# Table lookups by one-hot matmul: two float32r parts of three tables in place of three bfloat16 parts of four

## The chip, the cores and the metric

One core of a Trainium2 chip runs the whole kernel. The metric is device microseconds of one execution, outside the profiler; the engines are called TensorE (PE, with PEld for its weight loads), VectorE (DVE), ScalarE (ACT), GpSimd (POOL) and SyncE (SP), as the profile's abbreviations have them.

## What is computed

A recommender's pairwise attention over 26 embedded fields, for a batch of 2048:

```python
emb = jax.vmap(lambda tbl, idx: tbl[idx], in_axes=(0, 1), out_axes=1)(embed_tables, sparse)   # 2048 x 26 x 32
bi = emb[:, FIRST, :] * emb[:, SECOND, :]                     # 325 pairs of fields
a = jax.nn.relu(jnp.einsum('bpd,dh->bph', bi, att_w_w) + att_w_b)
scores = jnp.einsum('bph,ho->bpo', a, att_d_w) + att_d_b
att_weight = jax.nn.softmax(scores, axis=1)
att_out = jnp.sum(att_weight * bi, axis=1)
x = jnp.concatenate([att_out, dense], axis=-1)
out = jax.nn.sigmoid(x @ fin_w + fin_b)
```

Each of the 26 tables has 12,500 rows of 32 float32 values (128 bytes a row). All is float32.

## The kernel before

The batch is 16 tiles of 128 rows, worked in four *quads* of four tiles (`g` is the tile in the quad). A quad runs over the fields f = 0 to 25. Field f's rows for the four tiles stand side by side in `emb[:, f, :]`, are transposed by VectorE (L829 into PSUM as `turned`, L831 into SBUF as `emb_t`), and multiplied with all fields before f (L855); the products go into a ring of six groups of 16 pairs. TensorE multiplies each full group twice, by the attention weights (L491) and by the final weights (L501), both in float32 on four column tiles of 32; ScalarE applies the relu (L614) and TensorE reduces it to scores (L515). At a quad's end stand the softmax's maximum, exponentials and weighted sums (L891 to L946).

The rows of `emb` come in by three ways, and the change shifts work between them:

- **Gathers.** GpSimd issues one indirect DMA of 128 rows for each tile and field (L441), in the order of the fields. `gathers_of(f)` (L125) says how many of a quad's four tiles are gathered: 4 as a rule, fewer where another way serves a field. From the second quad on, GpSimd waits before field f until VectorE has transposed field f of the quad before (L435); so it can be up to one quad ahead. That makes 352 gathers, and L430 issues one more for field 24: 353.
- **Row copies.** For two tiles of field 24, SyncE copies single rows by their register addresses (L411): 128 DMAs a tile, 7 tiles (`TILES_SP`), 896 DMAs. The addresses are loaded 32 at a time (L407, 28 loads). ScalarE sets the rows into `emb` before field 24 (L656, `place_rows`).
- **Lookups.** Four fields (`LOOK = (3, 9, 15, 19)`) are looked up by TensorE: all four tiles of fields 3, 9 and 15, two tiles of field 19 (`LOOK_TILES`), 14 tiles a quad. The table lies in SBUF as 128 x 7 chunks of 14 rows; a one-hot matrix of the chunk numbers (L750, VectorE) times the table picks for each batch row its chunk of 14 x 32 = 448 values in PSUM (L476); `take_looked` masks the row wanted (L840) and sums over the 14 (L843). To be exact, the float32 table is split into three bfloat16 parts: `make_high` (L587, ScalarE rounds), `make_rest` (L757, VectorE subtracts), `make_middle` (L592, ScalarE rounds the rest), `make_low` (L762, VectorE subtracts). A tile takes 7 chunks x 3 parts = 21 matmuls, in two steps (chunks 0 to 3, chunks 4 to 6).

The order on TensorE is written out by hand: `STEP_FIELDS` lists beside which field each of a quad's lookup steps stands, and the first table of the next quad is looked up beside the end of this one. Before the first field, field 3 of quad 0 is looked up. SyncE loads the tables (L377 to L380): the first two at the start, the other two between its row copies, each after a wait that the ring's space, in which the raw table lies, has become free.

Of the kernel before, what the change touches and what calls it, by code (L numbers as in the profile page):

```python
# [5 lines left out]
P = 128  # L6
G = 4
# [16 lines left out]
LOOK = (3, 9, 15, 19)  # L24
LOOK_TILES = (4, 4, 4, 2)
CHUNKS = 7
CHUNK_ROWS = 14
PART_ROWS = CHUNKS * CHUNK_ROWS
CHUNK_DT = mybir.dt.float16
PARTS = 3  # L30
STEPS = (slice(0, 4), slice(4, 7))
STEP_FIELDS = (1, 2, 2, 3, 4, 4, 5, 6, 6, 7, 8, *range(8, 21), 22, 24)
SPLIT_FIELD = {2: 4, 3: 8}
# [14 lines left out]
def attention_fm(nc, dense, sparse, tables, params, look_index, sp_index, chunk_numbers, out):  # L48
    f32, i32, bf16 = mybir.dt.float32, mybir.dt.int32, mybir.dt.bfloat16
# [132 lines left out]
    with ctx:  # L182
# [19 lines left out]

        look_parts = sb("look_parts", [P, LOOKS, CHUNKS, PARTS, CHUNK_ROWS * D], bf16)

# [9 lines left out]
        onehot = sb("onehot", [P, CHUNKS, G * P], bf16)  # L214
# [75 lines left out]
        look_rest_made = [sem(f"look_rest_made{n}") for n in range(len(LOOK))]  # L290
        look_middle_made = [sem(f"look_middle_made{n}") for n in range(len(LOOK))]
# [73 lines left out]
        def _(sp):  # L365
# [27 lines left out]
            for q in range(QUADS):  # L393
                for i in range(PLACED - TILES_SP[q], PLACED):
# [3 lines left out]
                    for p in range(0, P, ROWS_SP):  # L398
# [5 lines left out]
                        if tiles == 0 and p == P // 2:  # L404
                            sp.wait_ge(look_low_made[1], len(STEPS))
                            load_table(3)
# [40 lines left out]
        def _(pe):  # L447
# [12 lines left out]
            for q in range(QUADS):  # L460

                def look_up(i):
                    of, n, g, part = steps[i]
                    made = (look_high_made[n], look_middle_made[n], look_low_made[n])
# [110 lines left out]
        def _(act):  # L575
# [14 lines left out]
            def make_middle(n, part):  # L590
                act.wait_ge(look_rest_made[n], part + 1)
                nc.scalar.activation(look_parts[:, n, STEPS[part], 1, :], raw[n][:, STEPS[part]], ACT.Copy  # L592
                                     ).then_inc(look_middle_made[n], 1)

# [6 lines left out]
            make_middle(0, 0)  # L601
            make_middle(0, 1)
            make_high(1, 0)
            make_high(1, 1)
            make_middle(1, 0)
            make_middle(1, 1)
            for q in range(QUADS):
# [51 lines left out]
                for f in range(1, F):  # L659
                    if f == SP_PLACE:  # L660
                        place_rows()
                    if q == 0:
                        for n in range(2, LOOKS):
                            for part in range(len(STEPS)):
                                if f == SPLIT_FIELD[n] - 1:
                                    make_high(n, part)
                                if f == SPLIT_FIELD[n] + 1:
                                    make_middle(n, part)
# [26 lines left out]
        def _(dve):  # L695
# [323 lines left out]
```

## Time and profile before

| | |
|---|---|
| runs, median | 479.75 us (478.36 to 480.0, 3 runs) |
| profiled execution, its span | 755.4 us; the page has no other time for it |
| TensorE busy | 489.4 us, 2788 instructions, mean granted clock 0.837 |
| VectorE busy | 419.0 us, 692 instructions |
| GpSimd busy | 343.8 us, 357 instructions |
| ScalarE busy | 118.3 us, 218 instructions |
| DMA moved | 15.60 MB in 15495 packets |

The profiled execution is one execution with the hardware profiler on; here it is over half as long again as the runs without it. A group's busy time is the sum of its instructions' durations; the number after the comma is the mean of one. TensorE's instructions overlap, so that its pace is read from the distance of starts, not from the duration of one. In the chain that ended last each row is a start, a length and what ran; "issue" is time in which nothing was waited for. In a timeline row the brackets hold the engine's idle time before and what ended it.

### The profile page before, as it was taken

The numbers are of one execution on the slowest core, as the hardware profiler recorded it, in microseconds if no ns is written. First come the engines' busy times: TensorE is split into PE (matmuls) and PEld (weight loads), VectorE is DVE, ScalarE is ACT, GpSimd is POOL, SyncE is SP. The second block draws the span as 40 slices with busy tenths as digits, with TensorE's granted clock in tenths as the row PEclk, the third lists the DMA queues.
The fourth block names the chain that finished last, engine by engine and source line by source line (L and its number), as shares of the span: only waits on it lengthen the run. The fifth ranks groups of instructions, "written<-read, shape, count | busy, mean of one in ns | idle before, by whom it ended". The sixth has DMA issues, their size and how long they took to land.

```text
span 755.4 us, 9968 instructions
## 1 busy us (share of the span) xinstructions
PE 489.4 (65%) x2788; PEld 175.7 (23%) x2788; DVE 419.0 (55%) x692; ACT 118.3 (16%) x218; POOL 343.8 (46%) x357
## 2 busy tenths in 40 slices
PE   2853102136686888737696898647687989999516
PEld 0321000012222233312232233212222224433102
DVE  6943003047475656444485666254476666899616
ACT  4211000003011123000011132000012132013114
POOL 6777777624745441744564541744564640000000
PEclk9985555559888899958898999868898999999958
DMA  7532521201211111111221110121221210000000
GB/s 234 120 18 13 99 13 12 13 3 9 13 8 12 8 10 33 12 8 10 11 11 10 10 10 4 13 37 9 11 12 9 12 10 2 2 2 2 0 1 1
DMA packets 15495, 15.60 MB, mean 21 GB/s; under 512 B 8177, under 2 KB 14161, under 8 KB 15057
## 3 DMA queue, kind: packets, MB, share of 16 engines
q0 software_dynamic: 11296, 5.81, 14.3%
q1 hardware_dynamic: 3488, 8.38, 3.1%
q10 hardware_dynamic: 656, 0.79, 0.4%
q8 instruction: 22, 0.36, 0.2%
q14 instruction: 33, 0.26, 0.1%
HBM read 14.93 MB, written 0.02 MB: 20 GB/s over the span
## 4 chain that ended last, share of the span: by engine, by line
SPq 59%; issue 38%; DVE 1%; PE 1%; DMA 1%; ACT 1%; ACTq 0%
SPq L411 51%; SPq L407 7%; DMA index<-look_index 0%; PE sums_s L515 0%; DVE ring L855 0%; PE sums_f L501 0%; PE first L491 0%; ACT score L685 0%; SPq L380 0%; DVE neg_max_early L891 0%; DMA emb_placed<-tables 0%; SPq L385 0%; ACT second_s L627 0%; ACT hidden L614 0%; PE back_s L538 0%
## 5 line engine op out<-in xcount | busy, mean ns | idle before, releaser
L441 POOL DMA_INDIRECT emb<-tables,rows x308 | 294.0, 955 | 261.0 <-DVE emb_t L831 164.6
L476 PE MATMUL looked_own<-look_parts,onehot 128*128 128x448 bf16 x735 | 178.8, 388 | 119.3 <-issue 75.3
L855 DVE TENSOR_TENSOR ring<-emb_t,turned 128x512 f32<-128x512 f32 (+9 forms) x180 | 193.9, 1114 | 3.4
L476 PE MATMUL back_s<-look_parts,onehot 128*128 128x448 bf16 x441 | 100.5, 380 | 73.2 <-issue 49.7
L614 ACT ACTIVATE hidden<-first,par 128x512 f32<-128x512 f32 (+1 forms) x84 | 56.4, 677 | 507.8 <-PE first L491 304.6
L476 PEld LDWEIGHTS looked_own<-look_parts,onehot 128*128 128x128 bf16 x735 | 72.7, 104 | 229.4 <-issue 158.9
L491 PE MATMUL first<-ring,par 128*32 128x512 f32 (+1 forms) x672 | 105.7, 616 | 22.6 <-DVE ring L855 8.2
L501 PE MATMUL sums_f<-ring,par 128*32 128x512 f32 (+1 forms) x672 | 105.7, 605 | 5.1 <-issue 4.2
L840 DVE TENSOR_TENSOR look_masked<-back_s,look_mask 128x448 f32<-128x448 f32 x21 | 13.0, 621 | 125.0 <-remote 70.8
L750 DVE TENSOR_TENSOR onehot<-chunk_of,turned 128x2048 bf16<-128x2048 f16 (+3 forms) x30 | 53.0, 1767 | 43.0 <-PE looked_own L476 26.4
L476 PEld LDWEIGHTS back_s<-look_parts,onehot 128*128 128x128 bf16 x441 | 43.6, 103 | 137.6 <-issue 79.8
L840 DVE TENSOR_TENSOR look_masked<-looked_own,look_mask 128x448 f32<-128x448 f32 x35 | 21.7, 621 | 96.2 <-remote 62.0
L441 POOL DMA_INDIRECT emb<-tables,rows_first x44 | 47.9, 1089 | 16.4 <-issue 13.1
L829 DVE STREAM_TRANSPOSE turned<-emb 128x128 f32<-128x128 f32 x100 | 31.9, 319 | 41.1 <-ACT emb L656 41.0
L515 PE MATMUL sums_s<-hidden,par 128*32 128x512 f32 (+1 forms) x168 | 29.0, 651 | 25.4 <-ACT hidden L614 25.4
L501 PEld LDWEIGHTS sums_f<-ring,par 128*32 128x32 f32 x672 | 26.4, 114 | 63.9 <-issue 61.8
L491 PEld LDWEIGHTS first<-ring,par 128*32 128x32 f32 x672 | 18.5, 109 | 74.9 <-issue 55.8
L843 DVE TENSOR_REDUCE emb<-look_masked 128x32 f32<-128x448 f32 x56 | 34.7, 620 | 1.9
L831 DVE STREAM_TRANSPOSE emb_t<-emb 128x128 f32<-128x128 f32 x100 | 27.1, 271 | 0.0
L592 ACT ACTIVATE look_parts<-ring 128x1792 bf16<-128x1792 f32 (+1 forms) x8 | 11.6, 1501 | 38.8 <-issue 26.2
L757 DVE TENSOR_TENSOR ring<-ring,look_parts 128x1792 f32<-128x1792 f32 (+1 forms) x8 | 14.1, 1790 | 3.5 <-issue 2.9
L515 PEld LDWEIGHTS sums_s<-hidden,par 128*32 128x32 f32 x168 | 5.6, 116 | 42.5 <-ACT hidden L614 34.2
(71 smaller groups left out, 145.0 us busy)
## 6 DMA issues: line engine op xcount, KB each, us to landing
emb_placed<-tables SPq DMA_DIRECT2D x896, 0.1 KB
emb<-tables,rows POOLq DMA_INDIRECT x308
ring<-tables SPq DMA_DIRECT2D x3, 1568.0 KB
chunk_of<-chunk_numbers SPq DMA_DIRECT2D x3, 512.0 KB, 3.6
ring<-tables SPq DMA_DIRECT2D x1, 896.0 KB
emb<-tables,rows_first POOLq DMA_INDIRECT x44
ring<-tables SPq DMA_DIRECT2D x1, 672.0 KB
chunk_of<-chunk_numbers ACTq DMA_DIRECT2D x1, 384.0 KB, 3.9
```

The costliest lines, as they stand in the source:

```text
L407: _, at = nc.values_load_multi_w_load_instructions(sp_rows[t:t + 1, p:p + ROWS_SP], engines=(mybir.EngineType.SP,), min_val=0, max_val=F * ...
L411: sp.dma_start(emb_placed[p + k:p + k + 1, q, i * D:(i + 1) * D], stacked[bass.ds(at[k], 1), :]).then_inc(sp_gathered[tiles], 16)
L441: pool.indirect_dma_start(emb[:, f, g * D:(g + 1) * D], None, stacked, bass.IndirectOffsetOnAxis(ap=row, axis=0), element_offset=at,).then ...
L476: mm = nc.tensor.matmul(looked_rows[look_bank[tile]], onehot[:, c, g * P:(g + 1) * P], look_parts[:, n, c, k, :], start=c == 0 and k == 0, ...
L491: mm = nc.tensor.matmul(first[gr % 2][j * TILE:(j + 1) * TILE, 0:n * P], w, ring[:, gr % RING, 0:n, j, :], start=True, stop=True)
L501: mm = nc.tensor.matmul(sums_f[j * TILE:(j + 1) * TILE, 0:pairs_c(gr) * P], row, ring[:, gr % RING, 0:pairs_c(gr), j, :], start=e == 0, st ...
L515: mm = nc.tensor.matmul(sums_s[tile * TILE:(tile + 1) * TILE, cut], d_sel[:, half, :], hidden[:, gr % HIDDEN, cut], start=half == 0, stop= ...
L614: nc.scalar.activation(hidden[:, gr % HIDDEN, cut], first[gr % 2][:, cut], ACT.Relu, bias=par[:, cols["bias_a"]]).then_inc(relu_done, 1)
L750: nc.vector.tensor_tensor(onehot[:, chunks, tiles], numbers.unsqueeze(1).broadcast_to(shape), here[:, chunks].unsqueeze(2).broadcast_to(sh ...
L840: nc.vector.tensor_tensor(look_masked[:], looked_rows[look_bank[tile]].rearrange("p (i d) -> p d i", d=D), mask, ALU.mult).then_inc(look_m ...
L843: nc.vector.tensor_reduce(emb[:, LOOK[n], g * D:(g + 1) * D], look_masked[:], AX.X, ALU.add).then_inc(look_summed, 1)
L855: nc.vector.tensor_tensor(slot[:, at:at + n, :], emb_t[:, i:i + n, :], turned[:, f % 2, :].unsqueeze(1).broadcast_to((P, n, P)), ALU.mult) ...
```

## The change

The tables are split into two parts of type float32r in place of three of bfloat16, and the one-hot matrix is float32r too. `make_rest` and `make_middle` go; `make_low` subtracts the high part from the raw table and writes the low part. A part has twice the bytes of before, so that two parts of three tables take the memory of three parts of four: field 19 is no longer looked up, and all four of its tiles are gathered. A quad has 12 looked-up tiles of 14 matmuls. `STEP_FIELDS` is drawn up anew for 22 + 2 steps. The descriptor memory for DMAs issued by GpSimd is set to 8192 bytes, where it had the default.

```diff
-LOOK = (3, 9, 15, 19)
-LOOK_TILES = (4, 4, 4, 2)
+LOOK = (3, 9, 15)
+LOOK_TILES = (4, 4, 4)
...
-PARTS = 3
+PARTS = 2
 STEPS = (slice(0, 4), slice(4, 7))
-STEP_FIELDS = (1, 2, 2, 3, 4, 4, 5, 6, 6, 7, 8, *range(8, 21), 22, 24)
-SPLIT_FIELD = {2: 4, 3: 8}
+STEP_FIELDS = (1, 2, 2, 3, 4, 4, 5, 6, 7, 8, 9, 10, 11, 12, 13, 13, 15, 17, 18, 20, 21, 23)
+SPLIT_FIELD = {2: 4}
+DMA_SCRATCH = 8192
...
-        look_parts = sb("look_parts", [P, LOOKS, CHUNKS, PARTS, CHUNK_ROWS * D], bf16)
+        look_parts = sb("look_parts", [P, LOOKS, CHUNKS, PARTS, CHUNK_ROWS * D], f32r)
...
-        onehot = sb("onehot", [P, CHUNKS, G * P], bf16)
+        onehot = sb("onehot", [P, CHUNKS, G * P], f32r)
...
-                        if tiles == 0 and p == P // 2:
-                            sp.wait_ge(look_low_made[1], len(STEPS))
-                            load_table(3)
...
-                    made = (look_high_made[n], look_middle_made[n], look_low_made[n])
+                    made = (look_high_made[n], look_low_made[n])
...
-            def make_middle(n, part):
-                act.wait_ge(look_rest_made[n], part + 1)
-                nc.scalar.activation(look_parts[:, n, STEPS[part], 1, :], raw[n][:, STEPS[part]], ACT.Copy
-                                     ).then_inc(look_middle_made[n], 1)
...
-            def make_rest(n, part):
+            def make_low(n, part):
                 dve.wait_ge(look_high_made[n], part + 1)
-                nc.vector.tensor_tensor(raw[n][:, STEPS[part]], raw[n][:, STEPS[part]], look_parts[:, n, STEPS[part], 0, :],
-                                        ALU.subtract).then_inc(look_rest_made[n], 1)
-
-            def make_low(n, part):
-                dve.wait_ge(look_middle_made[n], part + 1)
-                nc.vector.tensor_tensor(look_parts[:, n, STEPS[part], 2, :], raw[n][:, STEPS[part]],
-                                        look_parts[:, n, STEPS[part], 1, :], ALU.subtract).then_inc(look_low_made[n], 1)
+                nc.vector.tensor_tensor(look_parts[:, n, STEPS[part], 1, :], raw[n][:, STEPS[part]],
+                                        look_parts[:, n, STEPS[part], 0, :], ALU.subtract).then_inc(look_low_made[n], 1)
...
-    nc = bacc.Bacc("TRN2", target_bir_lowering=False, num_devices=1)
+    nc = bacc.Bacc("TRN2", target_bir_lowering=False, num_devices=1, dynamic_dma_scratch_size=DMA_SCRATCH)
```

## Rows read from the trace of the kernel before

**Rows 1.** The page: span, busy time, TensorE's clock, the chain's shares.

```profile
span 755.4 us, 9968 instructions
...
PE 489.4 (65%) x2788; PEld 175.7 (23%) x2788; DVE 419.0 (55%) x692; ACT 118.3 (16%) x218; POOL 343.8 (46%) x357
...
PEclk9985555559888899958898999868898999999958
...
SPq L411 51%; SPq L407 7%; DMA index<-look_index 0%; PE sums_s L515 0%; DVE ring L855 0%; PE sums_f L501 0%; PE first L491 0%; ACT score L685 0%; SPq L380 0%; DVE neg_max_early L891 0%; DMA emb_placed<-tables 0%; SPq L385 0%; ACT second_s L627 0%; ACT hidden L614 0%; PE back_s L538 0%
```

**Rows 2.** The chain that ended last: start, length; SyncE's register loads.

```profile
639.59 2.17 SPq L407
...
732.36 1.16 DMA emb_placed<-tables
```

**Rows 3.** The starts of GpSimd, SyncE and VectorE's fields (timeline, chain).

```profile
3.76 1.08 POOL L441 DMA_INDIRECT emb<-tables,rows_first  x1 [3.29 <-DVE rows_first L704]
...
8.04 2.07 SPq L407
...
37.59 0.30 DVE L831 STREAM_TRANSPOSE emb_t<-emb 128x128 f32<-128x128 f32 x1
```

**Rows 4.** Timeline of the end: field 24 placed, field 25 transposed.

```profile
733.63 0.26 ACT L656 ACTIVATE emb<-emb_placed 128x64 f32<-128x64 f32 x1 [26.44 <-DMA emb_placed<-tables]
...
740.98 0.32 DVE L829 STREAM_TRANSPOSE turned<-emb 128x128 f32<-128x128 f32 x1
```

**Rows 5.** Timeline of GpSimd where it waits for nothing.

```profile
79.75 0.94 POOL L441 DMA_INDIRECT emb<-tables,rows  x1 [0.30 <-issue]
81.00 0.94 POOL L441 DMA_INDIRECT emb<-tables,rows  x1 [0.30 <-issue]
```

**Rows 6.** Waits of GpSimd: us in total, times, longest.

```profile
POOL emb L441 <- DVE emb_t L831: 164.6, 27, 16.2
```

**Rows 7.** Groups by form, GpSimd's gathers: busy us, mean ns.

```profile
L441 POOL DMA_INDIRECT emb<-tables,rows x308 | 294.0, 955 | 261.0 <-DVE emb_t L831 164.6 <-issue 84.8 <-DVE turned L829 11.6
L441 POOL DMA_INDIRECT emb<-tables,rows_first x44 | 47.9, 1089 | 16.4 <-issue 13.1 <-DVE rows_first L704 3.3
L430 POOL DMA_INDIRECT emb_placed<-tables,rows x1 | 1.6, 1628 | 0.3 <-issue 0.3
```

**Rows 8.** Stretch of quad 3: PE, PEld, DVE, ACT, POOL busy, clock, DMA.

```profile
640.00:707.00 67.00, 65.36 (x450) 24.68 (x448) 62.51 (x97) 12.51 (x19) 0.00 (x0) 1.00 0.01 1
```

**Rows 9.** Timeline of TensorE's weight loads, two looked-up tiles.

```profile
473.95 3.88 PEld L476 LDWEIGHTS back_s<-look_parts,onehot 128*128 128x128 bf16 x21
...
477.92 2.56 PEld L476 LDWEIGHTS looked_own<-look_parts,onehot 128*128 128x128 bf16 x14
```

**Rows 10.** The same, two float32 groups.

```profile
690.30 0.13 PEld L491 LDWEIGHTS first<-ring,par 128*32 128x32 f32 x4 [0.30 <-issue]
...
691.16 0.13 PEld L515 LDWEIGHTS sums_s<-hidden,par 128*32 128x32 f32 x4 [0.30 <-ACT hidden L614]
```

**Rows 11.** Groups by form, VectorE; and one row of its timeline.

```profile
L843 DVE TENSOR_REDUCE emb<-look_masked 128x32 f32<-128x448 f32 x56 | 34.7, 620 | 1.9
...
L855 DVE TENSOR_TENSOR ring<-emb_t,turned 128x2048 f32<-128x2048 f32 x12 | 27.4, 2280 | 0.0
...
L750 DVE TENSOR_TENSOR onehot<-chunk_of,turned 128x2048 bf16<-128x2048 f16 x11 | 25.1, 2283 | 15.3 <-PE looked_own L476 15.2
L840 DVE TENSOR_TENSOR look_masked<-looked_own,look_mask 128x448 f32<-128x448 f32 x35 | 21.7, 621 | 96.2 <-remote 62.0 <-issue 17.0 <-PE looked_own L476 13.2
...
L750 DVE TENSOR_TENSOR onehot<-chunk_of,turned 128x1024 bf16<-128x1024 f16 x4 | 4.9, 1221 | 27.7 <-remote 16.5 <-PE looked_own L476 11.2
...
L750 DVE TENSOR_TENSOR onehot<-chunk_of,turned 128x768 bf16<-128x768 f16 x4 | 3.8, 944 | 0.0
...
L757 DVE TENSOR_TENSOR ring<-ring,look_parts 128x1792 f32<-128x1792 f32 (+1 forms) x8 | 14.1, 1790 | 3.5 <-issue 2.9 <-ACT look_parts L587 0.5
...
32.94 3.54 DVE L762 TENSOR_TENSOR look_parts<-ring,look_parts 128x1792 bf16<-128x1792 f32 x2
```

More of the change, by code:

```diff
@@ L48, in attention_fm @@
 def attention_fm(nc, dense, sparse, tables, params, look_index, sp_index, chunk_numbers, out):
-    f32, i32, bf16 = mybir.dt.float32, mybir.dt.int32, mybir.dt.bfloat16
+    f32, i32, f32r = mybir.dt.float32, mybir.dt.int32, mybir.dt.float32r
     ALU, ACT, AX = mybir.AluOpType, mybir.ActivationFunctionType, mybir.AxisListType
@@ L289, in attention_fm @@
         look_high_made = [sem(f"look_high_made{n}") for n in range(len(LOOK))]
-        look_rest_made = [sem(f"look_rest_made{n}") for n in range(len(LOOK))]
-        look_middle_made = [sem(f"look_middle_made{n}") for n in range(len(LOOK))]
         look_low_made = [sem(f"look_low_made{n}") for n in range(len(LOOK))]
@@ L600, in _ @@
             act.wait_ge(par_in, 16)
-            make_middle(0, 0)
-            make_middle(0, 1)
             make_high(1, 0)
             make_high(1, 1)
-            make_middle(1, 0)
-            make_middle(1, 1)
             for q in range(QUADS):
@@ L666, in _ @@
                                     make_high(n, part)
-                                if f == SPLIT_FIELD[n] + 1:
-                                    make_middle(n, part)
                     done = groups_of(f)
@@ L752, in make_onehots @@
                                         ).then_inc(onehot_made, 1)
-            def make_rest(n, part):
+            def make_low(n, part):
                 dve.wait_ge(look_high_made[n], part + 1)
-                nc.vector.tensor_tensor(raw[n][:, STEPS[part]], raw[n][:, STEPS[part]], look_parts[:, n, STEPS[part], 0, :],
-                                        ALU.subtract).then_inc(look_rest_made[n], 1)
-            def make_low(n, part):
-                dve.wait_ge(look_middle_made[n], part + 1)
-                nc.vector.tensor_tensor(look_parts[:, n, STEPS[part], 2, :], raw[n][:, STEPS[part]],
-                                        look_parts[:, n, STEPS[part], 1, :], ALU.subtract).then_inc(look_low_made[n], 1)
+                nc.vector.tensor_tensor(look_parts[:, n, STEPS[part], 1, :], raw[n][:, STEPS[part]],
+                                        look_parts[:, n, STEPS[part], 0, :], ALU.subtract).then_inc(look_low_made[n], 1)
             make_onehots(0, 0, 0)
-            make_rest(0, 0)
             make_onehots(0, 0, 1)
-            make_rest(0, 1)
             make_low(0, 0)
@@ L867, in _ @@
                                 if tile == 0:
-                                    make_rest(1, part)
-                                if tile == 1:
                                     make_low(1, part)
@@ L875, in _ @@
                                 if f == SPLIT_FIELD[n]:
-                                    make_rest(n, part)
-                                if f == SPLIT_FIELD[n] + 1:
                                     make_low(n, part)
```

## The prediction, written before the changed kernel was run

> **What bounds the kernel now.** The page's head comes first, because the time cannot be read from it directly: the profiled execution spans 755.4 us [rows 1] and the page gives it no other time, while the median of the runs is 479.75 us. So 276 us exist only under the profiler, and the first task is to find which rows still hold without it. The chain that ended last is SyncE's queue almost throughout: its two lines, 896 row copies of L411 and 28 register loads of L407, hold 58% of it, and nearly all the rest is the gaps between them [rows 1]. Late in the span, when GpSimd has nothing left to do, its steps become regular: six batches of 32 rows pass in (732.36 - 639.59) / 6 = 15.46 us each [rows 2], a register load of 2.17 us and so (15.46 - 2.17) / 32 = 0.415 us a row. I take 15.46 us as the pace without disturbance. SyncE starts at 8.04 [rows 3], so it needs 8.0 + 28 x 15.46 + some 2.5 us (an estimate, half a microsecond each) for the five table and chunk loads between = 443.4, 1.2 for the last row to land [rows 2], and 21.9 from field 24 in place (733.6) to the end (755.4) [rows 4]: 466.5 us.
>
> GpSimd next. Where it is not held it starts a gather every 1.25 us (79.75, 81.00), 0.945 busy and 0.30 before the next [rows 5]; in the profile it also waits 164.6 us in 27 places for VectorE to free a field's slot [rows 6], which is there because SyncE holds up the whole rest. Without those waits: 3.8 to its start [rows 3], busy 294.0 + 47.9 + 1.6 = 343.5 for 353 gathers [rows 7], 352 x 0.305 = 107.4 between; it ends at 454.7. About 1.2 to land (a row's landing) and 14.4 from field 25's transpose (740.98) to the end [rows 4]: 470 us.
>
> TensorE and VectorE last. From 640 to 707 quad 3 runs fields 0 to 23 with all data there: TensorE is busy 65.36 of 67.00 at a granted clock of 1.00 (2.4 GHz), VectorE 62.51 [rows 8]. That stretch has 10 looked-up tiles; quads 0 to 2 have 14, as they also make field 3 of the next quad. A tile of 21 matmuls takes 3.97 us (473.95 to 477.92) [rows 9], so four tiles are 16. Quad 3: 67.0 and 21.9 for the end = 89; quads 1 and 2: 105; quad 0, from VectorE's first field at 37.6 [rows 3], 105 + 14 of table splitting: it ends at 157. Sum 157 + 105 + 105 + 89 = 456 us.
>
> So three chains lie within 14 us of each other, GpSimd's longest: 470, 466.5, 456. All are short of 479.75. I put the 9.8 us left to what lies around the span, which no row here shows; the three are compared with each other, and the difference is laid on the median.
>
> **The change part by part.**
>
> *GpSimd.* Field 19 loses its table, so `gathers_of(19)` goes from 2 to 4: 2 more gathers in each of 4 quads, 353 to 361. At 1.25 us they are +10.0 us on a queue that in my reading never waits. What they free: nothing on this engine. Field 19 comes late by 2.5 us more per quad, and everything behind it on that queue too.
>
> *Descriptor memory.* It is set to 8192 bytes. Whether GpSimd ever waits for room there is not visible. Below: nothing, most gathers take 0.945. Above: a first-fields gather has a mean of 1089 ns against 955 for the others [rows 7]; if all 361 paid that 0.14, +50 us. I take nothing, as the undisturbed row is the one that repeats; a gain has no source, as the gathers already go back to back.
>
> *TensorE.* 14 tiles x 21 matmuls become 12 x 14 a quad: 1176 to 672. The price of one float32r matmul is on no row. From below: the bfloat16 matmul of the same shape and line, 3.97 / 21 = 0.189 us [rows 9]. From above: a float32 product of 512 columns comes as two instructions; a group of eight on four column tiles takes 0.86 us (690.30 to 691.16) [rows 10], so 448 columns would be 0.75, and half of it, one instruction, 0.376. I take 0.189, the row with the same tile and shape: a tile costs 2.65 us. A quad falls from 55.6 to 31.8 us of lookups. The new `STEP_FIELDS` lays 22 half tiles over fields 1 to 23, where 26 lay over 1 to 24. All of it lies beside GpSimd's 112 us a quad, so it is worth nothing while GpSimd is last. At 0.376 a tile costs 5.26 and a quad's lookups 63 us, 7.6 more than now; 4 quads put the TensorE chain at 456 + 30 = 486 before the splitting saved below, 468 after it, still under GpSimd's 480.
>
> The row of float32 shows 512 columns in 0.43 us per instruction, twice the time per column of bfloat16. The Trainium skill (SBUF — State Buffer, section "A bandwidth-pool intuition that's wrong (but worth ruling out)") puts TensorE's moving read at about 614 GB/s, stated for 2-byte data; 448 x 128 elements of 4 bytes would by it take an estimated 374 ns. It agrees with that row and speaks against this change: by it the lookups would cost more than before, and the sum would still be GpSimd's.
>
> *VectorE.* Gone: 8 `make_rest` (14.1 us), 2 of 8 `make_low` of the same size (3.5), the one-hots of the fourth table (4.9 + 3.8), and 8 of 56 `take_looked` at 0.62 + 0.62 (9.9) [rows 11]: 36.2 us of 419.0. The one-hots that stay write 4-byte elements; from below the row of today, 2.28 us for 2048, from above twice that, 24 x 2.0 = 48 us more. I take today's, because the float32 product of 2048 also takes 2.28 [rows 11]. `make_low` now waits for `make_high` itself; behind it stand the masks of the first tiles, and it comes earlier than today by the two steps that are gone.
>
> *ScalarE.* 8 `make_middle` and 2 `make_high` go, some 15 us on an engine busy 118.3 of 755.4 [rows 1]. It is never last; nothing.
>
> *SyncE.* One table load with its wait for `look_low_made[1]` goes, and the chunk loads shrink: under 1 us. Behind that wait stand 26 x 32 row copies, but the low part of table 1 is ready at 32.94 + 3.54 = 36.5 us [rows 11], before SyncE comes to it at 8 + 2 x 15.5 = 39; so it costs nothing today. SyncE's chain: 466.
>
> Sum: GpSimd 470 + 10 = 480, SyncE 466, TensorE and VectorE 456 - 18 of splitting - 3 quads x some 11 = 405. A quad's 105 would lose 24 of lookups, but VectorE's busy time, 419.0 - 36.2 with some 30 before the first field, leaves 88 a quad, and with its waits at a quad's end I keep 94. The longest grows by 10.0 us: 479.75 + 10 = 489.75, I say 489.5.
>
> **The rivals.** (1) *SyncE is last, GpSimd has slack.* For: its chain is only 3.5 us shorter, and an error of 1% in GpSimd's pitch turns the order. Against: SyncE's steady pace was itself taken under the profiler. It decides at a pitch of 1.22: 361 x 1.22 in place of 361 x 1.25 brings GpSimd's 480 to 469, within 2.5 of SyncE. Below that the ten microseconds vanish in the slack: 479 us, no change.
>
> (2) *TensorE and VectorE are last today.* It needs both queues to be faster than their rows: the 0.30 between gathers to shrink to 0.20 (1.15 a gather) and a copied row from 0.415 to 0.385. Then GpSimd after the change needs 480 - 361 x 0.10 = 444 and SyncE 466.5 - 896 x 0.03 = 440, and the TensorE chain, 456 plus stalls of some 8 for one-hots and masks, would have set today's time with 16 around it. After the change it no longer does: 444 + 16 = 460 us, faster. The point from which it decides is a pitch of 1.22 with SyncE as quick. For: TensorE is busy 489 us in the profile, more than the whole unprofiled time, part of it at the low clock [rows 1]. Against: in the dense stretch that clock is 1.00 [rows 8], and SyncE's copies, in regular steps there, show little added by tracing.
>
> (3) *float32r costs as float32*, 0.75 us a matmul: 10.5 us a tile, 48 x 10.5 = 504 us of lookups against 222; TensorE's chain 456 + 282 - 18 = 720, with the 9.8 around it 730 us. For: the elements have four bytes. Against: float32 comes as two instructions, and float32's is already the price of two passes over the same columns.
>
> **How the numbers follow.** Forecast 0.61, rival 1 0.16, rival 2 0.19, rival 3 0.04. A measurement of this kernel can tell about 0.5% (2.4 us) from no change. Faster 0.19, same 0.16, slower 0.65. The forecast's own range is 484 to 498: +4 where SyncE's chain takes most of it up, +18 if the 4-byte matmul and the descriptor memory add some microseconds. With rival 1 and the near side of rival 2 the range is 473 to 498.
>
> **What would show it.** The page after: 361 gathers at an unchanged pitch of 1.25, 672 lookup matmuls at 0.19 (0.38 or 0.75 by the others), `make_rest` gone, SyncE's steps of 15.46 unchanged. The profiled span should stay near 755, as SyncE's disturbed queue sets it; only the runs' time tells the chains apart. A time under 477 means that GpSimd's queue was not last; one over 500 that the float32r matmuls or the descriptor memory were priced too low.

## The result, and the profile after

| | runs, median | ratio to the kernel before | span of the profiled execution |
|---|---|---|---|
| before | 478.64 us (477.63 to 480.86, 12 runs) | | 476.3 us (a second profile) |
| after | 481.17 us (480.13 to 482.19, 12 runs) | 1.0050 (1.0036 to 1.0064) | 480.3 us |

The change makes the kernel slower by 0.5%, 2.5 us. The forecast was 489.5: the sign came true, and the size was a quarter of the one forecast (+2.5 where +10 was). 481.17 lies below the forecast's own range, 484 to 498; only the wider range, made for the rivals, holds it.

The execution profiled of the kernel before was stretched to 755.4 us [rows 1]. Profiled a second time it spans 476.3 us, in a run of 478.1; all comparisons below are with this second profile. The head of its page and its chain:

```profile
span 476.3 us, 9968 instructions
...
PE 424.1 (89%) x2788; PEld 166.1 (35%) x2788; DVE 418.2 (88%) x692; ACT 119.4 (25%) x218; POOL 346.4 (73%) x357
...
PE 50%; DVE 26%; issue 8%; POOL 7%; ACT 2%; DMA 2%; POOLq 0%; DVEq 0%
```

The same three parts of the page after:

```profile
span 480.3 us, 8890 instructions
...
PE 370.7 (77%) x2284; PEld 182.2 (38%) x2284; DVE 384.4 (80%) x654; ACT 105.5 (22%) x208; POOL 346.6 (72%) x365
...
POOL 69%; issue 22%; DMA 3%; DVE 3%; PE 2%; ACT 1%; POOLq 0%
```

TensorE is busy 53 us less, VectorE 34 us less, and GpSimd, with eight gathers more, 0.2 us more. The chain was one of TensorE and VectorE; now it is GpSimd's gathers from end to end. The waits say the same. VectorE's waits for gathers, before (second profile):

```profile
DVE turned L829 <- DMA emb<-tables,rows: 7.1, 5, 1.9
```

and after, with GpSimd's own waits:

```profile
DVE turned L807 <- DMA emb<-tables,rows: 65.8, 42, 3.5
...
POOL emb L437 <- issue: 108.5, 356, 0.3
...
POOL emb L437 <- DVE emb_t L809: 0.9, 3, 0.3
```

VectorE waits 65.8 us in 42 places where it waited 7.1 in 5: all that the lookups gave back has become waiting for gathers. GpSimd, once it has started, waits for VectorE 0.9 us in all; it issues from its first gather to its last, as the forecast had it. So the start of the last gather should tell the time. Timeline of GpSimd, the last one before (second profile) and after:

```profile
456.42 0.94 POOL L441 DMA_INDIRECT emb<-tables,rows  x1 [0.30 <-issue]
```

```profile
459.02 0.94 POOL L437 DMA_INDIRECT emb<-tables,rows  x1 [0.31 <-issue]
```

It starts 2.60 us later, and the medians of the times are 2.53 us apart. The two executions that were profiled lie further apart, 478.1 and 482.13, because 18.9 us stand behind the last gather's end before, and 20.3 after. TensorE in that stretch, before (second profile), then TensorE and VectorE after:

```profile
456.20 1.07 PE L491 MATMUL first<-ring,par 128*32 128x512 f32 x8 [0.28 <-DVE ring L855]
```

```profile
456.90 1.93 PE L487 MATMUL first<-ring,par 128*32 128x512 f32 x8 [1.67 <-DVE ring L833]
458.61 1.83 PE L497 MATMUL sums_f<-ring,par 128*32 128x512 f32 x8
...
464.75 1.22 DVE L865 TENSOR_REDUCE neg_max_early<-score 128x4 f32<-128x1024 f32 x1 [1.24 <-ACT score L629]
```

After the change the granted clock is 0.50 (1.2 GHz) from 453.4 to 460.2, behind a stretch in which TensorE had been idle for 2.46 us; the groups of eight matmuls take nearly twice as long, and VectorE waits 1.24 us for the scores that come of them. All twelve runs of the changed kernel have a lower mean clock (0.92 to 0.96) than the kernel before has in its runs (0.97 to 0.99). How much of the 2.53 us this makes is not shown; what follows is about the queue of gathers. Eight gathers at 1.25 us make 10.0, so 7.4 us must have gone from GpSimd's queue elsewhere. The groups by form show where from: gathers before (second profile), then after.

```profile
L441 POOL DMA_INDIRECT emb<-tables,rows x308 | 294.6, 956 | 93.9 <-issue 93.0 <-DVE emb_t L831 0.9
L441 POOL DMA_INDIRECT emb<-tables,rows_first x44 | 50.7, 1152 | 16.4 <-issue 13.1 <-DVE rows_first L704 3.3
```

```profile
L437 POOL DMA_INDIRECT emb<-tables,rows x316 | 298.4, 944 | 96.3 <-issue 95.4 <-DVE emb_t L809 0.9
L437 POOL DMA_INDIRECT emb<-tables,rows_first x44 | 47.0, 1069 | 16.5 <-issue 13.1 <-DVE rows_first L689 3.4
```

308 gathers fall from 956 to 944 ns in the mean (3.7 us), the 44 of the first fields from 1152 to 1069 (3.7 us): together the 7.4 that was missing. No gather became faster; a few slow ones went. GpSimd's timeline after, and VectorE's in the same microseconds:

```profile
10.23 0.94 POOL L437 DMA_INDIRECT emb<-tables,rows_first  x1 [0.31 <-issue]
11.48 2.47 POOL L437 DMA_INDIRECT emb<-tables,rows_first  x1 [0.30 <-issue]
14.25 1.16 POOL L437 DMA_INDIRECT emb<-tables,rows_first  x1 [0.30 <-issue]
15.71 0.94 POOL L437 DMA_INDIRECT emb<-tables,rows_first  x1 [0.30 <-issue]
```

```profile
9.45 1.75 DVE L735 TENSOR_TENSOR onehot<-first,par 128x1536 fp32r<-128x1536 f32 x1
11.11 3.48 DVE L742 TENSOR_TENSOR look_parts<-ring,look_parts 128x1792 fp32r<-128x1792 f32 x2
14.51 0.37 DVE L753 TENSOR_SCALAR clamped<-ids 128x416 f32<-128x416 int32 x1
```

The gathers at 11.48 and 14.25 take 2.47 and 1.16 us where their neighbours take 0.94, and both meet `make_low`, whose two operands (`ring` and `look_parts`) lie in SBUF. The one-hot of 1.75 us just before has one operand in PSUM (`first`), and the gather at 10.23 runs through it undelayed. Nearly all the time over 0.945 us stands at such places: at the sixteen `make_rest` and `make_low` before (12.7 us), at the six `make_low` after (5.2). I call what a gather takes above 0.945 us *held*, and sum it over all gathers, by the timeline's rows with their 0.01 us: 13.4 us before, 6.0 after, again 7.4 between them.

The float32r matmul is in TensorE's timeline (weight loads, two tiles of 14):

```profile
261.07 2.76 PEld L472 LDWEIGHTS back_s<-look_parts,onehot 128*128 128x128 f32 x14 [0.71 <-issue]
263.84 2.86 PEld L472 LDWEIGHTS looked_own<-look_parts,onehot 128*128 128x128 f32 x14
```

A tile takes 263.84 - 261.07 = 2.77 us, 0.198 a matmul, and the next one 2.86, 0.204, against 0.189 of bfloat16 [rows 9].

### The profile page after: what moved, and what is told of

Its sections match the earlier page's. It is cut to its first block, busy times and chain, and to the rows that moved or that the text cites. A ratio compares the mean times of both kernels' runs of the same rounds, so it can differ in the third digit from the quotient of the medians.

```text
span 480.3 us, 8890 instructions
## 1 busy us (share of the span) xinstructions
PE 370.7 (77%) x2284; PEld 182.2 (38%) x2284; DVE 384.4 (80%) x654; ACT 105.5 (22%) x208; POOL 346.6 (72%) x365
## 4 chain that ended last, share of the span: by engine, by line
POOL 69%; issue 22%; DMA 3%; DVE 3%; PE 2%; ACT 1%; POOLq 0%
POOL emb L437 68%; DMA emb<-tables,rows 2%; DVE ring L833 1%; PE first L487 1%; PE sums_f L497 1%; DMA ids<-sparse 0%; PE sums_s L511 0%; DVE turned L807 0%; ACT score L670 0%; POOLq L183 0%; DVE neg_max_early L865 0%; DVE emb_t L809 0%; POOL emb_placed L426 0%; ACT second_s L614 0%; PE back_s L534 0%
## 5 line engine op out<-in xcount | busy, mean ns | idle before, releaser
L487 PE MATMUL first<-ring,par 128*32 128x512 f32 (+1 forms) x672 | 97.0, 657 | 45.9 <-DVE ring L833 45.6
L472 PE MATMUL looked_own<-look_parts,onehot 128*128 128x448 f32 x420 | 104.8, 398 | 32.2 <-DVE onehot L735 14.7
L472 PEld LDWEIGHTS looked_own<-look_parts,onehot 128*128 128x128 f32 x420 | 81.6, 201 | 67.4 <-issue 37.0
L497 PE MATMUL sums_f<-ring,par 128*32 128x512 f32 (+1 forms) x672 | 95.8, 640 | 0.0
L807 DVE STREAM_TRANSPOSE turned<-emb 128x128 f32<-128x128 f32 x100 | 32.3, 323 | 70.1 <-DMA emb<-tables,rows 65.8
L472 PE MATMUL back_s<-look_parts,onehot 128*128 128x448 f32 x252 | 58.6, 378 | 17.8 <-DVE onehot L735 11.1
L472 PEld LDWEIGHTS back_s<-look_parts,onehot 128*128 128x128 f32 x252 | 45.7, 189 | 36.7 <-DVE onehot L735 18.3
L437 POOL DMA_INDIRECT emb<-tables,rows_first x44 | 47.0, 1069 | 16.5 <-issue 13.1
L735 DVE TENSOR_TENSOR onehot<-chunk_of,turned 128x2048 fp32r<-128x2048 f16 (+1 forms) x22 | 44.3, 2014 | 6.7 <-PE looked_own L472 6.7
L821 DVE TENSOR_REDUCE emb<-look_masked 128x32 f32<-128x448 f32 x48 | 29.8, 620 | 1.6
L583 ACT ACTIVATE look_parts<-ring 128x1792 fp32r<-128x1792 f32 (+1 forms) x6 | 8.8, 1507 | 16.1 <-DMA ring<-tables 16.0
L818 DVE TENSOR_TENSOR look_masked<-back_s,look_mask 128x448 f32<-128x448 f32 x18 | 11.1, 617 | 0.0
L614 ACT ACTIVATE second_s<-sums_s,par 128x512 f32<-128x512 f32 x12 | 8.3, 689 | 11.7 <-PE sums_s L511 11.7
```

The costliest lines, as they stand in the source:

```text
L437: pool.indirect_dma_start(emb[:, f, g * D:(g + 1) * D], None, stacked, bass.IndirectOffsetOnAxis(ap=row, axis=0), element_offset=at,).then ...
L472: mm = nc.tensor.matmul(looked_rows[look_bank[tile]], onehot[:, c, g * P:(g + 1) * P], look_parts[:, n, c, k, :], start=c == 0 and k == 0, ...
L487: mm = nc.tensor.matmul(first[gr % 2][j * TILE:(j + 1) * TILE, 0:n * P], w, ring[:, gr % RING, 0:n, j, :], start=True, stop=True)
L497: mm = nc.tensor.matmul(sums_f[j * TILE:(j + 1) * TILE, 0:pairs_c(gr) * P], row, ring[:, gr % RING, 0:pairs_c(gr), j, :], start=e == 0, st ...
L735: nc.vector.tensor_tensor(onehot[:, chunks, tiles], numbers.unsqueeze(1).broadcast_to(shape), here[:, chunks].unsqueeze(2).broadcast_to(sh ...
L807: tr = nc.vector.transpose(turned[:, f % 2, :], emb[:, f, :])
```

## The experiments

In one table what all runs gave. "Held" is the sum defined above, "waits" VectorE's for gathers of `rows`, as in the lines above. These and the last gather are of the one execution profiled, whose time lies up to 1.6 us from the median. The ratio is to the kernel before, run on the same chip in turn.

| kernel | gathers | last gather starts | held | waits | time | ratio (95%) |
|---|---|---|---|---|---|---|
| before, profiled again | 353 | 456.4 | 13.4 | 7.1 | 478.1 | |
| after | 361 | 459.0 | 6.0 | 65.8 | 481.17 | 1.0050 (1.0036 to 1.0064) |
| e1 three tables, bf16 | 361 | 463.1 | 10.1 | 53.9 | 486.37 | 1.0141 (1.0119 to 1.0164) |
| e2 two parts of three | 353 | 455.8 | 12.7 | 27.8 | 479.75 | 0.9997 (0.9979 to 1.0015) |
| e3 descriptor memory | 353 | 457.6 | 14.5 | 7.0 | 479.61 | 1.0005 (0.9988 to 1.0022) |
| e4 subtraction twice, SBUF | 361 | 460.7 | 7.6 | 59.8 | 483.65 | 1.0078 (1.0059 to 1.0098) |
| e5 the second from PSUM | 361 | 458.4 | 5.4 | 57.7 | 480.08 | 1.0019 (1.0002 to 1.0037) |
| e6 subtraction from PSUM | 361 | 454.7 | 1.7 | 61.2 | 476.5 | 0.9926 (0.9906 to 0.9945) |
| e7 before, no subtractions | 353 | 445.3 | 2.3 | 13.5 | 468.45 | 0.9762 (0.9744 to 0.9779) |
| e8 before, splits in PSUM | 353 | 449.1 | 6.1 | none | 477.85 | 0.9956 (0.9938 to 0.9973) |
| e9 after, in pieces | 361 | 456.9 | 3.9 | 66.4 | 479.02 | 0.9988 (0.9976 to 0.9999) |
| e10 before, in pieces | 353 | 450.8 | 7.7 | none | 473.93 | 0.9877 (0.9860 to 0.9894) |

**The kernel before, profiled again.** No edit.

> The kernel before, unchanged, for a second profile. The first one spans 755 us, and if the profiler happens to leave this one alone its span should be within 2 us of 478.6, as the changed kernel's is (480.3 beside 481.2). Theory A, TensorE and VectorE set the time of before: GpSimd ends its 353 gathers near 450 us, VectorE reaches the last fields later than their gathers land and waits for lookups, not for gathers; TensorE is busy over 95% in most of the span. Theory B, SyncE sets it: VectorE waits for field 24's copied rows at the quads' ends. Theory C, GpSimd sets it and its gathers were slower with the larger descriptor memory: gathers stand about 1.27 us apart and the last one lands near 462.

The span is 476.3 us and the time 478.1; the rows stand above. Only 1.8 us lie around the span. The chain of the page is that of theory A, while the gathers, 1.29 us apart in the mean, are rather those of theory C; its cause, the descriptor memory, is tried below.

**Three tables without float32r.** The gathers of the change alone: its table list, its steps and its loads, with three bfloat16 parts.

```diff
-LOOK = (3, 9, 15, 19)
-LOOK_TILES = (4, 4, 4, 2)
+LOOK = (3, 9, 15)
+LOOK_TILES = (4, 4, 4)
...
-                        if tiles == 0 and p == P // 2:
-                            sp.wait_ge(look_low_made[1], len(STEPS))
-                            load_table(3)
```

> Before with the three tables, 12 tiles and 361 gathers of the change, but still three bfloat16 parts. Theory A: TensorE loses 8 of 56 tiles (32 us of lookups), so GpSimd becomes last as in the changed kernel: 480.5 to 482, the float32r parts are then worth nothing. Theory B: the same, 481. Theory C: 478.6 + 10 = 488.6.

None of the three theories had it: the time grows by 6.8 us (486.37 against 479.59). On GpSimd's queue: +10.0 for eight gathers, -3.3 held, as the fourth table's four subtractions are gone; the last gather starts 6.6 us later. So the gathers cost what the forecast said, and the two float32r parts, which take six more subtractions away, give the rest back.

**Two parts of three.** A third of the lookup matmuls left out of the kernel before; all splitting stays.

```diff
-                    for k in range(PARTS):
+                    for k in range(PARTS - 1):
...
-                                                  stop=c == CHUNKS - 1 and k == PARTS - 1)
+                                                  stop=c == CHUNKS - 1 and k == PARTS - 2)
```

> Before with the third part's matmuls left out (14 instead of 21 a tile; the tables are still split in three, so the lowest part is missing from the looked-up rows); 353 gathers. Theory A: TensorE loses 392 matmuls, 74 us, and GpSimd's 353 gathers set the time: 481.2 - 8 x 1.25 = 471, 1.6% faster. Theory B and theory C: 478.6, no change.

Theory A's 471 is missed: 392 matmuls fewer change nothing (0.9997). GpSimd's last gather starts at 455.8, and VectorE's waits for gathers grow from 7.1 to 27.8 us. TensorE's chain is not the one that limits alone, for all that the page names it in the chain.

**Descriptor memory.** The kernel before with the change's setting.

```diff
-    nc = bacc.Bacc("TRN2", target_bir_lowering=False, num_devices=1)
+    nc = bacc.Bacc("TRN2", target_bir_lowering=False, num_devices=1, dynamic_dma_scratch_size=8192)
```

> Before with the descriptor memory of 8192 bytes alone. Theory A and theory B: 478.6, no change. Theory C: about 471, as the gathers get their 1.25 us.

1.0005, with the long gathers still where the subtractions are. The setting is not their cause, and theory C is out.

**The subtraction once more, with both operands in SBUF.** The changed kernel, with each `make_low` preceded by one of the same size into a spare tensor.

```diff
             def make_low(n, part):
                 dve.wait_ge(look_high_made[n], part + 1)
+                dve.wait_ge(spare_made, n * len(STEPS) + part)
...
+                nc.vector.tensor_tensor(spare, raw[n][:, STEPS[part]], look_parts[:, n, STEPS[part], 0, :], ALU.subtract
+                                        ).then_inc(spare_made, 1)
```

> The changed kernel with each of the six subtractions of make_low done once more into unused memory: both operands in SBUF, 10.7 us of VectorE in all. Theory L (GpSimd's gather is held up while VectorE subtracts two SBUF tensors): the gathers' time over 0.945 us each, 6.0 us in all in the changed kernel, about doubles to 11 to 12, the last gather starts 5 us later (464) and the time is 486. Theory M (the table loads' DMA traffic slows the early gathers): the excess stays at 6, the time 481.2. Theory N (VectorE's own time matters at the start): later first field by some 7 us, but the time stays within 1 us, as GpSimd is last.

**The same, with one operand in PSUM.** The edit is shown against the kernel just above.

```diff
-                nc.vector.tensor_tensor(spare, raw[n][:, STEPS[part]], look_parts[:, n, STEPS[part], 0, :], ALU.subtract
+                nc.vector.tensor_tensor(spare, chunk_first[:, 0:CHUNK_ROWS * D].unsqueeze(1).broadcast_to((P, count, CHUNK_ROWS * D)), look_parts[:, n, STEPS[part], 0, :], ALU.subtract
                                         ).then_inc(spare_made, 1)
```

> The same six extra subtractions of the same size, but one operand is read from PSUM. Theory L: the excess stays at 6.0 us, the last gather near 459, the time 481.2: same VectorE time as in the run before, no loss. Theory M: 481.2 in both. If any long VectorE instruction held up a gather, both would come to 486.

Twelve subtractions of SBUF tensors: 483.65. Six and six from PSUM, of the same length on VectorE: 480.08, no more than the changed kernel. So it is not VectorE's work but where its operands lie. Theories M and N, which had no change for the first, are out. Of theory L's effect the time has half (+2.5 us on the changed kernel where 5 was expected), and held grows by 1.6 us where it should have doubled. The timelines say why. VectorE, then GpSimd, in the kernel with the second from PSUM:

```profile
11.08 2.01 DVE L747 TENSOR_TENSOR hidden<-first,look_parts 128x1792 f32<-128x1792 f32 x1
13.01 2.01 DVE L749 TENSOR_TENSOR look_parts<-ring,look_parts 128x1792 fp32r<-128x1792 f32 x1
14.95 1.55 DVE L747 TENSOR_TENSOR hidden<-first,look_parts 128x1344 f32<-128x1344 f32 x1
16.41 1.55 DVE L749 TENSOR_TENSOR look_parts<-ring,look_parts 128x1344 fp32r<-128x1344 f32 x1
17.88 0.37 DVE L760 TENSOR_SCALAR clamped<-ids 128x416 f32<-128x416 int32 x1
```

```profile
11.44 0.94 POOL L438 DMA_INDIRECT emb<-tables,rows_first  x1 [0.30 <-issue]
12.69 0.95 POOL L438 DMA_INDIRECT emb<-tables,rows_first  x1 [0.30 <-issue]
13.94 1.91 POOL L438 DMA_INDIRECT emb<-tables,rows_first  x1 [0.30 <-issue]
16.15 0.94 POOL L438 DMA_INDIRECT emb<-tables,rows_first  x1 [0.31 <-issue]
17.40 1.38 POOL L438 DMA_INDIRECT emb<-tables,rows_first  x1 [0.30 <-issue]
```

The gathers at 11.44 and 12.69 start within the subtraction from PSUM and take 0.94 and 0.95. Those at 13.94 and 17.40 start within one of SBUF tensors; they end at 15.85 and 18.78, each 0.90 us behind the start of VectorE's next instruction (14.95, 17.88). And this holds where the next one is of SBUF tensors again. VectorE, then GpSimd, with both operands in SBUF:

```profile
25.79 2.02 DVE L747 TENSOR_TENSOR hidden<-ring,look_parts 128x1792 f32<-128x1792 f32 x1
27.73 2.02 DVE L749 TENSOR_TENSOR look_parts<-ring,look_parts 128x1792 fp32r<-128x1792 f32 x1
29.66 1.55 DVE L747 TENSOR_TENSOR hidden<-ring,look_parts 128x1344 f32<-128x1344 f32 x1
```

```profile
25.85 2.78 POOL L438 DMA_INDIRECT emb<-tables,rows_first  x1 [0.30 <-issue]
28.93 1.63 POOL L438 DMA_INDIRECT emb<-tables,rows_first  x1 [0.30 <-issue]
```

28.63 is 0.90 behind 27.73, and 30.56 is 0.90 behind 29.66. In a row of such instructions one gather gets through at each boundary, so each costs what it lasts beyond 1.25 us (1.93 or 1.47 from start to start): 0.7 or 0.2 us, not a whole hold. Six extra ones make some 2.7 by that, and the difference between the two kernels, in the start of the last gather, is 2.3.

What lets a gather go on is the end of the subtraction, and not the next instruction. Mostly the next one starts 0.08 or 0.09 us before that end by the records, but in the run on descriptor memory VectorE stands idle behind one. VectorE, then GpSimd:

```profile
14.18 1.55 DVE L757 TENSOR_TENSOR ring<-ring,look_parts 128x1344 f32<-128x1344 f32 x1
16.36 2.02 DVE L762 TENSOR_TENSOR look_parts<-ring,look_parts 128x1792 bf16<-128x1792 f32 x1 [0.63 <-ACT look_parts L592]
```

```profile
14.96 1.58 POOL L441 DMA_INDIRECT emb<-tables,rows_first  x1 [0.30 <-issue]
```

The gather ends at 16.54, 0.81 us behind the subtraction's end (15.73) and only 0.18 behind the next start. One kind of gather gets through: one that starts together with the subtraction. From the kernel with both operands in SBUF:

```profile
11.41 2.06 DVE L747 TENSOR_TENSOR hidden<-ring,look_parts 128x1792 f32<-128x1792 f32 x1 [0.18 <-ACT look_parts L584]
13.39 2.01 DVE L749 TENSOR_TENSOR look_parts<-ring,look_parts 128x1792 fp32r<-128x1792 f32 x1
```

```profile
11.41 0.94 POOL L438 DMA_INDIRECT emb<-tables,rows_first  x1 [0.30 <-issue]
```

Here the gather takes its 0.94 us, and VectorE is 0.05 longer. Over all runs of the table, 122 gathers start within a subtraction of two SBUF tensors: 115 are held and end 0.81 to 0.82 us behind its end, and seven, which start in its first 0.02 us, are not held. Of 39 that start within a subtraction with one operand in PSUM none is held.

**The subtraction from PSUM.** ScalarE copies the raw table, chunk by chunk, into PSUM banks that are free at the time, and `make_low` reads it there; of the edit `make_low` is shown.

```diff
-                nc.vector.tensor_tensor(look_parts[:, n, STEPS[part], 1, :], raw[n][:, STEPS[part]],
-                                        look_parts[:, n, STEPS[part], 0, :], ALU.subtract).then_inc(look_low_made[n], 1)
+                for c in range(STEPS[part].start, STEPS[part].stop):
+                    dve.wait_ge(raw_copied, n * CHUNKS + c + 1)
+                    sub = nc.vector.tensor_tensor(look_parts[:, n, c, 1, :], raw_bank(part, c),
+                                                  look_parts[:, n, c, 0, :], ALU.subtract)
+                sub.then_inc(look_low_made[n], 1)
```

> The changed kernel with the raw table copied to free PSUM banks by ScalarE, chunk by chunk, and make_low reading it there: no subtraction has two SBUF operands any more. Theory L: the excess falls from 6.0 to about 1, the last gather starts near 454, the time is 476 to 477, under both kernels (478.6 and 481.2). Theory M: 481.2, or later by what the longer splitting costs at the start.

476.5 us, as theory L had it: by the ratios 0.7% under the kernel before and 1.2% under the changed one. Held falls to 1.7, and the last gather starts at 454.7. Page, chain:

```profile
POOL 68%; issue 22%; DVE 3%; DMA 3%; PE 2%; ACT 1%; POOLq 0%
```

GpSimd is still last. This kernel has also cut the subtraction into pieces; the last two runs part the two.

**No subtractions.** The kernel before without its subtractions, and so without their holds; it leaves the splitting of the tables out.

```diff
-                act.wait_ge(look_rest_made[n], part + 1)
                 nc.scalar.activation(look_parts[:, n, STEPS[part], 1, :], raw[n][:, STEPS[part]], ACT.Copy
                                      ).then_inc(look_middle_made[n], 1)
+                nc.scalar.activation(look_parts[:, n, STEPS[part], 2, :], raw[n][:, STEPS[part]], ACT.Copy
+                                     ).then_inc(look_low_made[n], 1)
...
-            def make_rest(n, part):
...
-            def make_low(n, part):
```

> The kernel before with all sixteen subtractions that split the tables left out of VectorE: ScalarE copies the raw table in the place of the remainder and of the low part, so the splitting itself is not computed; tiles, matmuls (21 for a tile) and gathers (353) are as before. Theory B (each subtraction between two tensors in SBUF holds GpSimd's gather that falls into it, 13.4 us in all over 353 gathers in the second profile of the kernel before): the gathers' excess falls to 1 or 2 us, the last gather starts at about 444 to 446 us instead of 456.4, and the time is 466 to 469 us where GpSimd stays last. If TensorE with VectorE is close behind, as their few waits for gathers in that profile say, the time stops short of that, at 469 to 474 us, with VectorE waiting for no gather. Were the long gathers due to anything else than these subtractions: 353 gathers with their excess kept, 477 to 480 us.

The last gather starts 11.1 us sooner, held falls by 11.1, and the time is 468.45, 2.4% below the kernel before, within the range expected. Of the 2.3 us of held time that stay, 1.2 stand at eight gathers, and the rest is a few ns at each of the others, with the rounding of the rows. GpSimd is not last here, as the expectation had it: SyncE's copies make up 70% of the chain that ended last. The third chain of the forecast is reached.

**The kernel before with its splits in PSUM.** As above for tables 0 to 2, the remainder formed in place; `make_rest` shown.

```diff
             def make_rest(n, part):
+                if n < 3:
+                    for c in range(STEPS[part].start, STEPS[part].stop):
+                        dve.wait_ge(raw_copied, n * CHUNKS + c + 1)
+                        sub = nc.vector.tensor_tensor(raw_bank(part, c), raw_bank(part, c), look_parts[:, n, c, 0, :],
+                                                      ALU.subtract)
+                    sub.then_inc(look_rest_made[n], 1)
+                    return
```

> The kernel before (three bf16 parts, four tables, 14 tiles, 353 gathers) with the splits of tables 0, 1 and 2 done in PSUM: ScalarE copies the raw table chunk by chunk into four banks that are free in that time, the remainder is formed there in place, and both subtractions have one operand in PSUM; those of table 3 stay between two tensors in SBUF. Theory B: the excess of the gathers falls from 13.4 us to 5 or 6 (some 2 us that a kernel without any subtraction keeps, and 3.6 us at table 3's four), the last gather starts at about 449 us, and the time is 470 to 473 us, below the changed kernel with its subtraction from PSUM (476.5), which has eight gathers more. Rival: without the long gathers TensorE and VectorE set the end, as VectorE has to do the subtractions still and chunk by chunk: 474 to 477 us, VectorE waiting for no gather. Were the operand in PSUM of no use here: 479 to 481 us.

A miss for the time, and in the mechanism the rival's case, though above its range too (474 to 477). Held falls to 6.1 and the last gather starts at 449.1, both as expected, but the time is 477.85. VectorE waits for no gather, and the chain reads:

```profile
PE 57%; DVE 29%; issue 5%; ACT 3%; DVEq 0%
```

Once the gathers come sooner, TensorE and VectorE set the end of the kernel before; the longer way through PSUM also brings its first field later (VectorE transposes it at 43.7 us, and at 37.8 in the kernel before; it waits 3.0 us for ScalarE's copies and 3.9 for its middle parts).

**The subtractions in pieces.** The changed kernel, then the kernel before; each subtraction cut into its chunks of 448 columns, all operands in SBUF.

```diff
-                nc.vector.tensor_tensor(look_parts[:, n, STEPS[part], 1, :], raw[n][:, STEPS[part]],
-                                        look_parts[:, n, STEPS[part], 0, :], ALU.subtract).then_inc(look_low_made[n], 1)
+                for c in range(STEPS[part].start, STEPS[part].stop):
+                    sub = nc.vector.tensor_tensor(look_parts[:, n, c, 1, :], raw[n][:, c],
+                                                  look_parts[:, n, c, 0, :], ALU.subtract)
+                sub.then_inc(look_low_made[n], 1)
```

> The changed kernel with each make_low subtraction cut into its chunks of 448 columns, both operands in SBUF as before (six instructions become twenty-one). In the profiles so far a long gather ends 0.90 us behind a boundary between two VectorE instructions (subtractions at 11.11 of 1.94 and 1.54 us; gathers 11.48 + 2.47 = 13.95 and 14.25 + 1.16 = 15.41). Theory B1, a gather waits only for the end of the VectorE instruction that it meets, and then runs beside the next one: pieces of some 0.53 us hold it by at most that, the excess falls from 6.0 us to 2 or 3, the last gather starts at 455 to 456 us, and the time is 477 to 478.5 us. Theory B2, the gather needs its whole time free of subtractions between SBUF tensors: cutting helps nothing, excess 6 us or more, 481 to 483 us; then the shorter time of the version with its operand in PSUM (476.5) came from PSUM and not from the cutting that it also had.

> The kernel before with its sixteen subtractions cut into chunks of 448 columns, all operands in SBUF as before (sixteen instructions become fifty-six). Theory B1: the excess falls from 13.4 us to about 5, and the last gather starts at 448 to 449 us; TensorE with VectorE then sets the end, as in the version with its splits in PSUM (477.85), so 475 to 478 us, and VectorE waits for no gather. Theory B2: excess and time stay, 479 to 481 us, with the last gather at 456 us or later.

VectorE, then GpSimd, in the changed kernel with pieces:

```profile
11.14 3.83 DVE L743 TENSOR_TENSOR look_parts<-ring,look_parts 128x448 fp32r<-128x448 f32 x7
```

```profile
11.41 1.16 POOL L437 DMA_INDIRECT emb<-tables,rows_first  x1 [0.30 <-issue]
12.88 1.31 POOL L437 DMA_INDIRECT emb<-tables,rows_first  x1 [0.30 <-issue]
14.49 1.30 POOL L437 DMA_INDIRECT emb<-tables,rows_first  x1 [0.30 <-issue]
```

None of these gathers is held by more than 0.37 us, where the first one here was held 1.53 us. Held falls from 6.0 to 3.9 and from 13.4 to 7.7, less than I put down (2 to 3, and 5), since three gathers meet a piece where two met a subtraction: in the kernel before 16 gathers are held at the subtractions for 12.7 us in all, and with pieces 19 for 6.0. Theory B1 is right and B2 out; the times are 479.02, above the range given, and 473.93, below it. The second is the fastest kernel here that leaves nothing out: 1.2% under the kernel before, from cutting sixteen instructions into fifty-six. Its chain is TensorE's and VectorE's (61% and 27%), and VectorE waits for no gather, so its gathers have no more to give. For the changed kernel, pieces alone reach 0.9988 of the kernel before, and pieces with one operand in PSUM 0.9926: cutting makes the first half of the way from 1.0050, and PSUM the second.

## Why the prediction was right or wrong

**GpSimd, +10.0: right.** 361 gathers at the old pitch, 0.9 us of waits for VectorE, SyncE not last: it waits at the end for VectorE, 34.4 us after (29.8 before).

**The step that failed** is the one on descriptor memory, with the sentence on VectorE's saving beside it. The forecast saw that the first fields' gathers take 1089 ns where the others take 955 [rows 7], put the difference down as the upper bound of descriptor memory, and wrote that "a gain has no source, as the gathers already go back to back". Back to back they go, but some were held while `make_rest` and `make_low` ran. These subtractions were costed at what VectorE gets back from them, worth nothing while GpSimd is last, while GpSimd pays for them: ten of sixteen went, and with them 7.4 of the 10.0 us. The sign came true only because 10.0 is more than 7.4, a term that the forecast did not have. A mean that is 14% above another of the same operation was the row to open, and the forecast's own sum had the amount: 353 gathers at 0.945 are 333.6 us, and it added up 343.5. The timeline of GpSimd holds the long ones one by one, and VectorE's timeline of the same microseconds names what holds them, in the stretched trace too:

```profile
28.56 2.63 POOL L441 DMA_INDIRECT emb<-tables,rows_first  x1 [0.30 <-issue]
```

```profile
28.35 3.48 DVE L757 TENSOR_TENSOR ring<-ring,look_parts 128x1792 f32<-128x1792 f32 x2
```

**"9.8 us around the span": wrong.** It is 1.8 (478.1 against 476.3). GpSimd's last gather ends at 457.4, not 454.7, and 18.9 us follow it, not 15.6: VectorE transposes field 25 only at 461.9, as it has the products of fields 23 and 24 to work off first. The three terms (2.7, 3.3 and 1.8) carry 470 to 478.1. The 1.2 us for a gather to land was a row copy's; the page of the second profile has 3.4 us from a gather's issue to its landing (median). The sign that the profiled span would stay near 755 failed as well, as the stretch did not come again.

**TensorE and VectorE, 456: too low.** With no wait for a gather they take the splits in pieces to a span of 472.3, within 4 us of the kernel before. By VectorE's first transposition in each quad, quad 0 ends at 166.4 there where 157 was taken, quads 1 and 2 take 106.2 each (105), and quad 3 with the end 93.5 (89). The forecast's second rival was thus nearly level, though not by its own condition, a pitch of 1.15, which stayed 1.25: that chain was as long as GpSimd's to some microseconds, and the page's chain of the second profile names it. It did not set the time alone, as the run with two parts of three shows, and a change that relieves one of two level chains and loads the other gains nothing from the first.

**SyncE, 466.5: right.** Without the subtractions its last row lands at 446.0 us (444.6 taken), and the span is 466.2.

**float32r: right.** 0.20 us a matmul against 0.189 taken; the estimate of 374 ns worked out from the Trainium skill (SBUF — State Buffer, "A bandwidth-pool intuition that's wrong (but worth ruling out)") and rival 3's 0.75 did not come about. The one-hots keep their 2.28 us, and VectorE saves 34 us (36.2 taken).

**Descriptor memory: nothing,** as taken (1.0005).

## What to carry to other kernels

Where an engine issues back to back and sets the time, look at each group's mean against its shortest rows: long single instances are time of that engine that another engine may own, and work removed there pays though it lies beside. Keep long VectorE instructions on two SBUF tensors away from a GpSimd queue that gathers, or cut them, or bring one operand from PSUM. And when a profiled span is far from the runs' time, chains that were put together from its rows have errors of their own, here 0, 6 and 16 us (466.5 against 466.2, 470 against 476.3, 456 against 472.3), so that a gap of 14 us between them decides little.

## What the runs showed of the hardware

A gather that starts within one of these subtractions with two inputs in SBUF, later than its first 0.02 us, ends 0.81 to 0.82 us behind the subtraction's end (115 cases; 2.78 us at most, against 0.945), whatever VectorE does next, and between two such subtractions too. One that starts within the first 0.02 us is not held (7 cases), and the subtraction is 0.05 us longer. With one input in PSUM no gather is held (39 cases, 0.94 or 0.95 us). VectorE is not longer for a held gather: its subtraction takes 2.02 us beside one, and 2.01 where one operand is in PSUM. The Trainium skill (SBUF — State Buffer, "Who interferes with whom") says that a VectorE instruction with two SBUF inputs contends with a GpSimd instruction that reads SBUF, and infers that the writing of descriptors is not stalled by such a `tensor_tensor`. The first half agrees with the runs; the gather as a whole is held all the same. That the 0.81 us are its descriptors and the held part the reading of its row numbers would fit both, and no run here shows it.

A float32r weight load takes 0.19 to 0.20 us (means of 189 and 201 ns in the groups) where bfloat16 took 0.10, and the matmuls follow at that pace. Of two profiled executions of one kernel one spanned 476 us and the other 755, and 32 of SyncE's row copies with their load took 15.2 to 16.7 us each time in the first and 15.3 to 77.8 in the second; what stretched it is not shown.

Left open: how the time moves with TensorE's granted clock at the end of the kernel, and how far splits in pieces would go with TensorE relieved; neither was tried.
